# A Mamba-style layer with an expert FFN: both batches' scans as one stream of 64 chunks, with projection, normalisation and output stage as side work at fixed chunks

## The chip, the cores and the metric

The kernel runs on one core of one Trainium2 chip. The metric is the device time of one execution in microseconds. Of the kernel before there are three timed runs, and one more execution was profiled.

## What is computed

x is (2, 2048, 128) in fp32, two batches of 2048 tokens. A small vector per batch (the modulation) gives shifts, scales and two gates ga and gb, whose magnitude is at least 0.25.

```
h = layernorm(x) * (1 + ca) + sa
zxbcdt = h @ in_proj_w.T                     # z 256, x 256, B 64, C 64, dt 2
per direction (forward, and backward on the reversed sequence):
    xBC = silu(causal_conv4(xBC)); dt = softplus(dt + dt_bias); A = -exp(A_log)
    state = state * exp(dt * A) + dt * x B^T;  y = C state + D * x    # per head
    y = y * silu(z);  y = y * rsqrt(mean(y*y) + eps) * norm_w
x = x + ga * ((y_fw + y_bw) @ out_proj_w.T)
h = layernorm(x) * (1 + cb) + sb
expert = argmax(h @ gate_w.T + gate_b + expert_bias)              # of 8
x = x + gb * (relu(h @ w1[expert] + b1) @ w2[expert] + b2)
```

## The kernel before, in words

Everything is one function, `build`, with one instruction list per engine written out by hand: SP issues loads, POOL is GpSimd, ACT ScalarE, PE TensorE, DVE VectorE. Each engine runs its list in order; an instruction that needs another's result waits on a counting semaphore (`wait_ge`). There is no scheduler: the order of the calls in the loops is the order of the work.

The sequence of a batch is cut into 16 chunks of 128 tokens, and four chunks make a block (512 tokens) or, in the scan, a step. A batch is scanned backwards first and then forwards, so it has 32 chunks in 8 steps. For each of the two batches, three phases follow one another, and each ends in `phase_end` (L325), at which all four engines drain and wait for each other:

- Phase 0, normalisation and projection. DVE takes statistics of all 16 chunks (L1075, L1078), POOL the power -1/2 (L477), DVE normalises (L1086), PE transposes (L809), ACT modulates (L606), PE projects to x, B and C (L819) and to z and dt (L825), DVE copies the former to `raw` (L1096), ACT takes silu of z (L617). Then come softplus (L1109 to L1131), the sums of decays (L832, L835), their exponentials (L626) and a split into three bf16 parts, `eparts` (L1147 to L1154). At the head of the second batch POOL also cuts b2 into parts (`cut_b2`, L449) before it does anything for phase 0.
- Phase 1, the scan. Convolution by step: for the two x groups ACT writes the first tap to PSUM banks 1 and 7 (`tap0`, L645) and DVE adds three (`taps`, L1168), the two banks in alternation; for B and C ACT and POOL do it in SBUF in two alternating accumulators (L636, L498, L503). ACT takes the tanh (L653, L656), DVE multiplies (`gate_bc` L1174, `gate_x` L1181), ACT copies C (L662). Per chunk: POOL makes `lseg` (L486); PE `prepare` (L847) transposes x and B and makes the score and decay matrices; ACT takes `decays` (L683), `tokens_major` (L673, L675) and `squares` (L691); DVE does `mix` (L1193, L1196), `carry` of the state (L1210) and `gate_y` (L1236); PE `scan` (L874) makes the new state's part in bank 6 and y in bank 4 or 5. PE is one chunk ahead: `prepare(q + 1)`, then `scan(q)`. `xt` and `bs` have three buffers (TM, L148).
- Phase 2, the output, in four blocks: ACT scales the forward part (L732), DVE adds the backward part (L1248), PE transposes (L915), ACT copies (L740), PE projects (L924), DVE multiplies by ga (L1301) and adds x (L1307), takes statistics (L1310, L1313), POOL the power (L549), DVE normalises (L1319, L1323), POOL shifts (L551), PE transposes (L951), ACT copies (L759), PE makes the gate's logits (L958), DVE chooses an expert (`choose`, L1261 to L1269), PE counts ranks (L934, L935), DVE computes each token's row (`place`, L1280 to L1291), and POOL scatters the four chunks of a block by four indirect DMAs (L538).

After both batches come tables of what each expert got (L1340 to L1363, padding rows by L569), and then the FFN: 39 tiles of 128 rows, loaded by expert, with L984 and L1001 as its matmuls and an indirect store (L582). The change leaves that part as it is, but for its place in memory.

PSUM banks are given by phase: in the scan 0 for transposes, 1 and 7 for the convolution, 2 and 3 for scores, 4 and 5 for y, 6 for the state.

## Time and profile before

| | us |
|---|---|
| three timed runs | 640.8, 639.4, 640.35 (median 640.35) |
| the profiled execution, its own time | 637.29 |
| its span, first to last instruction | 635.4 |
| mean granted TensorE clock | 0.802 of full speed |
| busy in the span: PE, DVE, POOL, ACT | 421.7, 395.9, 301.4, 270.9 |

The time of an execution holds some 1.9 us more than the span of its instructions. Terms of a sum are taken from the profiled execution, and the sum is set beside 637.29 before it is set beside the median. The page gives busy time by engine; a view by stage gives the same for stretches of the span, with the granted clock (1.00 is 2.4 GHz, 0.50 is 1.2); the view by line gives the mean duration of an instruction and, where neighbours overlap on an engine, a busy time that is less than count times mean.

### The profile page before, as it was taken

Reading aid. Unit: us, or ns where it says so; the run is one execution under the profiler, and the core shown is the slowest. Engines: PE = TensorE matmul, PEld = TensorE weight load, DVE = VectorE, ACT = ScalarE, POOL = GpSimd, SP = SyncE. Lnnn points to the kernel's source line nnn. Section 1 sums busy time; section 2 is a strip of 40 time slices with the busy share of each in tenths; the row PEclk is TensorE's granted clock in tenths of the full one; section 3 lists DMA queues with packets and bytes.
Section 4 is the critical chain, followed back from the end, with each engine's and each line's share of the span. In section 5 each row is a group of like instructions: output and inputs, shape, how many; then the busy total and the mean of one; then the engine's idle time right before and its main releaser. Section 6 shows DMA issues by size and latency. Waiting matters only on the chain.

```text
span 635.4 us, 9951 instructions
## 1 busy us (share of the span) xinstructions
PE 421.7 (66%) x2798; PEld 360.9 (57%) x2798; DVE 395.9 (62%) x1240; ACT 270.9 (43%) x777; POOL 301.4 (47%) x453
## 2 busy tenths in 40 slices
PE   0329329998998575306627999999667310799994
PEld 0116218877887474204416878788556310799994
DVE  0365476888884474524556888886476424387884
ACT  1014456777774421003626777775521000344441
POOL 7410087656643154472037666672125454165664
PEclk9959658999999755557956999999875555699997
DMA  8300000000000001000000000000000014488780
GB/s 221 132 1 0 1 1 2 1 1 2 1 2 2 0 26 42 34 34 0 1 1 0 2 2 1 2 2 2 1 1 34 34 68 123 131 231 229 210 237 26
DMA packets 20789, 29.16 MB, mean 46 GB/s; under 512 B 4076, under 2 KB 13548, under 8 KB 20608
## 3 DMA queue, kind: packets, MB, share of 16 engines
q1 hardware_dynamic: 17520, 20.98, 11.9%
q0 software_dynamic: 3216, 7.56, 3.3%
q8 instruction: 23, 0.38, 0.3%
q14 instruction: 30, 0.25, 0.1%
HBM read 20.97 MB, written 8.01 MB: 46 GB/s over the span
## 4 chain that ended last, share of the span: by engine, by line
PE 27%; DVE 25%; POOL 14%; issue 14%; ACT 10%; DMA 4%; POOLq 2%; SPq 2%; DVEq 0%; ACTq 0%
DVE bank L1168 6%; PE bank L819 4%; POOL routed_rows L538 3%; DVE ms L1193 3%; DMA out_dram<-arena 2%; ACT bank L645 2%; DVE st L1210 2%; POOLq L327 2%; PE bank L984 2%; PE bank L825 2%; POOL out_dram L582 2%; PE bank L870 2%; DVE bc L1174 2%; PE bank L890 2%; ACT es L683 2%
## 5 line engine op out<-in xcount | busy, mean ns | idle before, releaser
L486 POOL TENSOR_SCALAR lseg<-strict,av 128x128 f32<-128x128 f32 x128 | 46.9, 380 | 69.3 <-PE bank L870 69.3
L1168 DVE SCALAR_TENSOR_TENSOR bank<-arena,cw,bank 128x512 f32<-128x512 f32 x96 | 65.8, 746 | 5.7 <-ACT bank L645 5.7
L498 POOL TENSOR_SCALAR prod<-arena,cw 128x512 f32<-128x512 f32 x48 | 33.2, 691 | 74.5 <-DVEq L327 73.7
L1193 DVE SCALAR_TENSOR_TENSOR ms<-es,dtv,bank 128x128 f32<-128x128 f32 x128 | 38.7, 343 | 37.4 <-ACT es L683 37.4
L582 POOL DMA_INDIRECT out_dram<-arena x39 | 38.4, 985 | 36.2 <-DVE arena L1399 16.0
L858 PE MATMUL bank<-ident,cx 128*128 128x128 f32 x128 | 26.0, 287 | 30.3 <-ACT cc L663 27.6
L883 PE MATMUL bank<-xt,bs 128*128 128x128 f32 x240 | 38.4, 284 | 9.9 <-DVE st L1210 9.9
L1001 PE MATMUL bank<-w2s,arena 128*128 x312 | 43.9, 285 | 0.0
L984 PE MATMUL bank<-arena 128*128 128x128 f32 x312 | 42.9, 282 | 0.0
L767 ACT ACTIVATE arena<-bank 128x128 f32<-128x128 f32 x39 | 10.8, 277 | 72.5 <-PE bank L973 70.6
L538 POOL DMA_INDIRECT routed_rows<-rows,rowat x32 | 31.8, 993 | 19.8 <-issue 14.9
L683 ACT ACTIVATE es<-bank 128x256 f32<-128x256 f32 x64 | 24.6, 385 | 38.3 <-PE bank L870 37.7
L870 PE MATMUL bank<-incl,lseg 128*128 128x128 f32 x256 | 40.7, 284 | 0.0
L858 PEld LDWEIGHTS bank<-ident,cx 128*128 128x128 f32 x128 | 16.9, 145 | 40.9 <-issue 32.9
L890 PE MATMUL bank<-xt,skip 128*128 128x128 f32 x256 | 40.1, 280 | 0.0
L894 PE MATMUL bank<-xt,ms 128*128 128x128 f32 x256 | 39.9, 279 | 0.0
L984 PEld LDWEIGHTS bank<-arena 128*128 128x128 f32 x312 | 39.6, 199 | 0.0
L1376 DVE TENSOR_SCALAR arena<-bank,arena 128x128 f32<-128x128 f32 x78 | 23.8, 346 | 24.9 <-PE bank L984 24.7
L883 PEld LDWEIGHTS bank<-xt,bs 128*128 128x128 f32 x240 | 32.5, 196 | 11.9 <-issue 11.9
L1001 PEld LDWEIGHTS bank<-w2s,arena 128*128 128x128 f32 x312 | 38.8, 196 | 0.5
L898 PE MATMUL bank<-st,cs 128*128 128x256 f32 x128 | 38.5, 382 | 0.0
L870 PEld LDWEIGHTS bank<-incl,lseg 128*128 128x128 f32 x256 | 35.6, 201 | 0.0
(223 smaller groups left out, 1203.3 us busy)
## 6 DMA issues: line engine op xcount, KB each, us to landing
arena<-in_w_dram SPq DMA_DIRECT2D x39, 258.0 KB, 3.5
arena<-routed_rows SPq DMA_DIRECT2D x39, 130.0 KB, 3.1
xs<-in_u_dram SPq DMA_DIRECT2D x4, 512.0 KB, 5.7
w2s<-in_w_dram SPq DMA_DIRECT2D x1, 2048.0 KB, 8.5
out_dram<-arena POOLq DMA_INDIRECT x39
routed_rows<-rows,rowat POOLq DMA_INDIRECT x32, 2.5
arena<-in_wmod_dram SPq DMA_DIRECT2D x1, 384.0 KB, 3.9
b2r<-in_b_dram SPq DMA_DIRECT2D x1, 384.0 KB, 9.2
```

Of the source, the lines that this page charges most:

```text
L486: last = pool.tensor_scalar(lseg[:, q % 2, h, :], strict[:, d, :], av[:, col(d, h, t)], 1.0, ALU.mult, ALU.mult)
L538: pool.indirect_dma_start(routed[:, :], bass.IndirectOffsetOnAxis(ap=rowat[:, k, :].bitcast(mybir.dt.uint32), axis=0), rows[:, k, :], None ...
L582: pool.indirect_dma_start(out_rows, bass.IndirectOffsetOnAxis(ap=tok[:, s % 4, :].bitcast(mybir.dt.uint32), axis=0), ob[:, s % 4, :], None ...
L858: pe.transpose(tx[:, h * HD:(h + 1) * HD], cx[:, s % 2, h, c0:c0 + P], ident[:, :])
L870: last = pe.matmul(sg[:, h * P:(h + 1) * P], lseg[:, q % 2, h, :], incl[:, d, :], start=False, stop=True, skip_group_check=True)
L883: last = pe.matmul(sn[:, h * HD:(h + 1) * HD], bs[:, q % TM, h].rearrange("p g n -> p (g n)"), xt[:, q % TM, h * HD:(h + 1) * HD], start=T ...
L890: pe.matmul(ys[:, h * HD:(h + 1) * HD], skip[:, d * NH + h, :], xt[:, q % TM, h * HD:(h + 1) * HD], start=(h == 0), stop=False, skip_group ...
L894: pe.matmul(ys[:, h * HD:(h + 1) * HD], ms[:, q % 2, h, :], xt[:, q % TM, h * HD:(h + 1) * HD], start=False, stop=False, skip_group_check= ...
L984: mm = pe.matmul(bank[2 + 2 * (s % 2) + f // 2][:, c0:c0 + P], w1b[:, s % RW, f * P:(f + 1) * P], hTs[:, s % 2, :], start=True, stop=True)
L1001: last = pe.matmul(y, hr[:, s % 2, f * P:(f + 1) * P], w2s[:, bass.ds(e, 1), f, :].rearrange("p a c -> p (a c)"), start=False, stop=(f == ...
L1168: dve.scalar_tensor_tensor(out=pacc[g][:, :], in0=raw[:, g, c0:c0 + BLK], scalar=cw[:, d, g, k:k + 1], in1=pacc[g][:, :], op0=ALU.mult, op ...
L1193: dve.scalar_tensor_tensor(out=ms[:, q % 2, h, :], in0=es[:, q % 2, h, :], scalar=dtv[:, col(d, h, t)], in1=sg[:, DI:DI + P], op0=ALU.mult ...
```

## The change

The chunks of both batches are numbered 0 to 63 and steps 0 to 15, and there is one loop over all of them. `phase_end` is left once only, ahead of the tables. What were phases 0 and 2 become side work that each engine does between chunks, at places fixed by step S and chunk j of the step:

- Blocks 0 and 1 of the first batch are projected ahead of the loop; 2 and 3 in steps 0 and 1; the second batch's in steps 6 to 9. The statistics of the second batch stand in steps 2 and 3 of the first, its softplus, sums and splits in steps 4 to 6. Statistics go by block (with one small power of -1/2 each) rather than by batch. `hT` has four buffers, not two, and dt is made for all 16 chunks at once.
- The output of a block is spread over three steps: forward norms, `forward`, `both`, `y_turn`, `out_proj`, `residual`, `second_deviation` in the step after its chunks; `second_norm`, `shift`, `h2_turn`, `logits`, `choose`, `ranks`, `place` in the next; `scatter` in the third. The last blocks' is done after the loop. Only two rounds of `rows` exist, as before, but each block's four scatters count on one semaphore.
- All side products of PE go through banks 6 and 7 in turn, in an order that a function lists (`side_order`); PE waits before use u for the reader of use u - 2 (`take`).
- The convolution's x groups go one after the other through bank 1 alone, B and C through one accumulator. `gate_x` is in two halves, chunks apart. The state's part shares bank 4 or 5 with y, so that `carry(Q)` waits for all of y(Q). TM is 2.
- ACT, not DVE, copies `raw`. silu of z is tanh(z/2) on ACT and (1 + t) z on DVE (twice silu; a factor 1/4 in the norm and 1/2 in the weights undo it). ga is multiplied into the output weights, so that L1301 is gone.
- At the start, DVE fills constants that POOL filled; SP loads c_t, half of the first batch, wmod, the other half, the projection weights, nine small operands, then the second batch and w2. The gates of the rows move into step 1, cut_b2 into step 3.

The diff is long; its core, new functions and the loops' order:

```diff
+def proj_at(S):
+    b, s = divmod(S, STEPS)
+    if s < 2:
+        return NBLK * b + s + 2
+    if s >= 6 and b + 1 < B:
+        return NBLK * (b + 1) + s - 6
+    return None
+def gate_at(S):
+    return 1 if S == 0 else proj_at(S - 1)
+def out_at(S, lag):
+    b, s = divmod(S - lag, STEPS)
+    if S < lag:
+        return None
+    if s > NBLK:
+        return NBLK * b + s - NBLK - 1
+    return NBLK * b - 1 if s == 0 and b >= 1 else None
...
+        def side(u):
+            return bank[6 + u % 2]
+        def take(eng, u):
+            if u >= 2:
+                eng.wait_ge(s_free[u % 2], u // 2)
...
-        TM = 3
+        TM = 2
...
-        pacc = (bank[1], bank[7])
...
         @block.gpsimd
+            for Q in range(NCH):
+                S, j = divmod(Q, BT)
+                b, s = divmod(S, STEPS)
+                if Q + 2 < NCH:
+                    decay_rows(Q + 2)
+                if j == 0 and out_at(S, 0) is not None:
+                    forward_norms(out_at(S, 0))
+                if j == 0 and S + 1 < NSTEP:
+                    taps_bc(S + 1, 1)
+                if j == 1 and S + 1 < NSTEP:
+                    taps_bc(S + 1, 0)
+                if j == 3 and S + 2 < NSTEP:
+                    raw_bc_there(S + 2)
+                    taps_bc(S + 2, 2)
...
+                if s in (2, 3) and b + 1 < B and j in (0, 2):
+                    reciprocal_deviation(NBLK * (b + 1) + 2 * (s - 2) + j // 2)
+                if j == 3 and out_at(S, 0) is not None:
+                    second_deviation(out_at(S, 0))
+                if j == 0 and out_at(S, 1) is not None:
+                    shift(out_at(S, 1))
+                if j == 0 and out_at(S, 2) is not None:
+                    scatter(out_at(S, 2))
+                if S == 3 and j == 2:
                     cut_b2()
+            scatter(LASTG - 2)
+            shift(LASTG - 1)
+            forward_norms(LASTG)
+            second_deviation(LASTG)
+            scatter(LASTG - 1)
+            shift(LASTG)
+            scatter(LASTG)
+            phase_end(pool)
...
         @block.scalar
+            for Q in range(NCH):
...
+                if Q + 1 < NCH:
+                    tokens_major(Q + 1)
+                    decays(Q + 1)
+                if Q >= 1:
+                    squares(Q - 1)
+                if S + 1 < NSTEP:
+                    if j == 0:
+                        tanh_x(S + 1, 0)
+                    if j == 1:
+                        tap0_x(S + 1, 1)
+                    if j == 2:
+                        tanh_bc(S + 1)
+                        tanh_x(S + 1, 1)
+                        two_c(S + 1)
+                if A is not None and j == 0:
+                    keep_raw(A, 2)
+                    keep_raw(A, 0)
+                if S + 2 < NSTEP and j == 2:
+                    tap0_bc(S + 2)
+                if S + 2 < NSTEP and j == 3:
+                    tap0_x(S + 2, 0)
...
         @block.tensor
...
+            def scan(Q):
...
+                ys = bank[4 + Q % 2]
+                sn = ys[:, DI:2 * DI]
...
+            for Q in range(NCH):
...
+                A, A1, g, g1 = proj_at(S), gate_at(S), out_at(S, 0), out_at(S, 1)
...
+                if Q + 1 < NCH:
+                    prepare(Q + 1)
+                scan(Q)
+                if A is not None and j == 0:
+                    project(A, 2)
+                    project(A, 0)
+                if A is not None and j == 1:
+                    project(A, 1)
+                if g1 is not None and j == 1:
+                    h2_turn(g1)
+                if A1 is not None and j == 1:
+                    project_z(A1, 0)
+                if g is not None and j == 2:
+                    y_turn(g, 0)
+                    y_turn(g, 1)
+                if g1 is not None and j == 2:
+                    logits(g1)
+                if g is not None and j == 3:
+                    out_proj(g)
+                if g1 is not None and j == 3:
+                    ranks(g1)
+                if A1 is not None and j == 3:
+                    project_z(A1, 1)
...
         @block.vector
+            def carry(Q):
+                dve.wait_ge(s_ys, Q + 1)
...
+            def taps_x(S, g):
...
+                X = NH * S + g
                 for k in (2, 1, 0):
...
+                    if k == HALO - 1:
+                        dve.wait_ge(s_tap0, X + 1)
+                    else:
+                        dve.wait_ge(s_tap, HALO * X + HALO - 1 - k)
+                    dve.scalar_tensor_tensor(out=bank[1][:, :], in0=raw[:, g, c0:c0 + BLK],
...
+            for Q in range(NCH):
...
+                if S + 1 < NSTEP and j == 0:
+                    taps_x(S + 1, 0)
+                if S + 1 < NSTEP and j == 1:
+                    gate_x(S + 1, 0)
+                if Q + 1 < NCH:
+                    mix(Q + 1)
+                carry(Q)
+                if S + 1 < NSTEP and j == 2:
+                    gate_bc(S + 1)
+                    gate_x(S + 1, 1)
+                gate_y(Q)
+                if S + 1 < NSTEP and j == 1:
+                    taps_x(S + 1, 1)
+                if S == 1 and j == 3:
+                    gates_of_rows()
...
+                if g1 is not None and j == 0:
+                    second_norm(g1)
+                if g is not None and j == 1:
+                    both(g)
+                if A1 is not None and j == 1:
+                    gate_z(A1, 0)
+                if g1 is not None and j == 2:
+                    choose(g1)
+                if g is not None and j == 3:
+                    residual(g)
+                if g1 is not None and j == 3:
+                    place(g1)
+                if A1 is not None and j == 3:
+                    gate_z(A1, 1)
```

## Rows read from the trace of the kernel before

**Rows 1.** The profile's page, busy us by engine, share of the span, instructions

```profile
PE 421.7 (66%) x2798; PEld 360.9 (57%) x2798; DVE 395.9 (62%) x1240; ACT 270.9 (43%) x777; POOL 301.4 (47%) x453
```

**Rows 2.** Busy time by stage: stretch, its length, each engine, granted clock, DMA share, GB/s

```profile
0.00:36.00 36.00, 5.10 (x12) 3.03 (x12) 9.45 (x42) 2.98 (x4) 20.23 (x47) 0.94 0.52 156
36.00:81.00 45.00, 24.99 (x90) 15.93 (x90) 24.41 (x97) 16.17 (x45) 3.14 (x2) 0.73 0.00 1
...
90.40:204.90 114.50, 108.03 (x792) 91.66 (x792) 91.41 (x222) 80.61 (x245) 68.14 (x107) 0.96 0.01 1
...
277.00:287.50 10.50, 0.00 (x0) 0.00 (x0) 4.26 (x32) 0.00 (x0) 9.12 (x11) 0.50 0.00 0
287.50:327.00 39.50, 24.47 (x90) 15.75 (x90) 19.93 (x64) 16.11 (x44) 3.11 (x2) 0.76 0.00 1
327.00:336.60 9.60, 0.00 (x0) 0.00 (x0) 6.09 (x10) 5.79 (x9) 8.64 (x12) 0.50 0.00 0
...
451.30:517.00 65.70, 34.61 (x160) 31.20 (x160) 35.30 (x133) 13.81 (x30) 25.13 (x31) 0.58 0.07 25
```

**Rows 3.** Busy time in four chunks of the first loop, columns as above

```profile
116.50:130.50 14.00, 13.15 (x103) 11.16 (x102) 12.33 (x30) 10.74 (x33) 8.62 (x15) 1.00 0.00 1
```

**Rows 4.** The second batch's output stage in order of time: start, us, engine, line

```profile
452.05 1.70 ACT L732 ACTIVATE cx<-arena,rn 128x256 f32<-128x256 f32 x4 [0.17 <-ACTq L327]
...
473.46 0.19 DVE L1261 TENSOR_TENSOR lg<-bank,gb_sum 128x32 f32<-128x32 f32 x1 [0.19 <-PE bank L958]
...
479.40 1.24 POOL L538 DMA_INDIRECT routed_rows<-rows,rowat  x1 [1.26 <-issue]
...
519.62 0.96 POOL L538 DMA_INDIRECT routed_rows<-rows,rowat  x1 [0.30 <-issue]
...
523.30 0.17 DVE L1340 TENSOR_TENSOR count<-nextrow,region 128x8 f32<-128x8 f32 x1 [8.30 <-POOL arena L565]
```

**Rows 5.** The start and the first phase 0 in order of time

```profile
15.43 0.20 ACT L596 ACTIVATE csil<-ct_in 128x2 f32<-128x2 f32 x1 [13.35 <-DMA arena<-in_wmod_dram]
...
66.55 0.29 DVE L1109 TENSOR_TENSOR arena<-dtr,biasb 128x32 f32<-128x32 f32 x2 [1.53 <-ACT dtr L618]
...
80.66 0.22 DVE L1154 CAST eparts<-arena 32x128 bf16<-32x128 f32 x1
```

**Rows 6.** PE's matmuls of the start and of a projected block, in order of time

```profile
24.58 0.98 PE L794 MATMUL bank<-csil,arena 128*128 128x2 f32 x4 [24.58 <-DVE arena L1029]
...
57.24 2.74 PE L819 MATMUL bank<-hT,wx 128*128 128x512 f32 x6
...
59.82 1.90 PE L825 MATMUL bank<-wz,hT 128*128 128x258 f32 x8
```

**Rows 7.** Groups by line: count, busy us, mean ns, idle before and its releaser

```profile
L1168 DVE SCALAR_TENSOR_TENSOR bank<-arena,cw,bank 128x512 f32<-128x512 f32 x96 | 65.8, 746 | 5.7 <-ACT bank L645 5.7
L1181 DVE SCALAR_TENSOR_TENSOR cx<-cx,bank 128x512 f32<-128x512 f32 x32 | 20.4, 675 | 0.0
L1096 DVE COPY arena<-bank 128x512 f32<-128x512 f32 x24 | 16.6, 692 | 16.7 <-PE bank L819 16.7
L1301 DVE TENSOR_TENSOR acc<-bank,row 128x512 f32<-128x512 f32 x8 | 5.5, 687 | 7.8 <-PE bank L924 7.8
L740 ACT ACTIVATE acc<-bank 128x512 f32<-128x512 f32 x16 | 8.7, 595 | 24.8 <-PE bank L915 24.8
```

**Rows 8.** Single lines: duration in ns, least, median and most, first and last start

```profile
L1174 DVE SCALAR_TENSOR_TENSOR bc<-bc,acc x8: 695/1292/1302, 88.1 to 418.6; 128x512 f32<-128x512 f32 x8
L1248 DVE SCALAR_TENSOR_TENSOR cx<-arena,rn,cx x32: 471/479/1487, 207.9 to 479.6; 128x256 f32<-128x256 f32 x32
L503 POOL TENSOR_TENSOR acc<-acc,prod x24: 1259/1272/1817, 81.8 to 408.4; 128x512 f32<-128x512 f32 x24
```

**Rows 9.** PE in order of time: the transposes that open the second and third chunk

```profile
94.39 0.69 PE L858 MATMUL bank<-ident,cx 128*128 128x128 f32 x2 [1.16 <-ACT bs L675]
...
100.21 0.38 PE L858 MATMUL bank<-ident,cx 128*128 128x128 f32 x2
```

More of the change, by code:

```diff
@@ L56, in build @@
+USE = {}
+for _key in side_order():
+    USE[_key] = len(USE)
 def build(nc, u, w_xbc, w_zdt, conv_w, conv_b, dt_bias, a_log, d_skip, norm_w, w_out, gate_w, gate_b,
@@ new lines, in _ @@
+            modulate(0)
+            modulate(1)
+            act.wait_ge(s_scaled, 1)
+            keep_raw(0, 2)
+            tap0_bc(0)
+            keep_raw(0, 0)
+            tap0_x(0, 0)
+            keep_raw(0, 1)
+            modulate(2)
+            for g in (2, 0, 1):
+                keep_raw(1, g)
+            modulate(3)
+            act.wait_ge(s_pmod, 2)
+            for b in range(B):
+                last = act.activation(row[:, b, :, :], bank[2 + b][:, :].rearrange("p (k c) -> p k c", k=4), ACT.Copy)
@@ new lines, in h2_turn, with logits @@
+            def h2_turn(g):
+                u = USE["h2", g]
+                take(pe, u)
+                pe.wait_ge(s_h2, g + 1)
+                for j in range(BT):
+                    last = pe.transpose(side(u)[:, j * P:(j + 1) * P], rows[:, (g % RB) * BT + j, 0:DM], ident[:, :])
+                last.then_inc(s_full[u % 2], 1)
+            def logits(g):
+                u = USE["lg", g]
+                take(pe, u)
+                wait_free(pe, USE["h2", g])
+                for j in range(BT):
+                    last = pe.matmul(side(u)[:, j * NE:(j + 1) * NE], h2c[:, j, :], gw[:, :], start=True, stop=True)
+                last.then_inc(s_full[u % 2], 1)
@@ new lines, in ranks @@
+            def ranks(g):
+                u = USE["rk", g]
+                take(pe, u)
+                pe.wait_ge(s_hot, g + 1)
+                V = BT * NE
+                hv = hot[:, g % 2].rearrange("p j e -> p (j e)")
+                pe.matmul(side(u)[:, 0:V], strict[:, 1, :], hv, start=True, stop=True)
+                pe.matmul(side(u)[:, V:2 * V], ones[:, :], hv, start=True, stop=True).then_inc(s_full[u % 2], 1)
+            pe.wait_ge(s_csbc, 1)
+            pe.wait_ge(s_mod, 32)
+            for m in range(2):
+                last = pe.matmul(bank[0][:, m * B:(m + 1) * B], wm[:, m * DM:(m + 1) * DM], csil[:, :], start=True, stop=True)
@@ new lines, in _ @@
+            last.then_inc(s_pmod, 1)
+            pe.wait_ge(s_const, 2)
+            turn(0)
+            for b in range(B):
+                last = pe.matmul(bank[2 + b][:, :], csil_bc[:, b, :], wm[:, 2 * DM:6 * DM], start=True, stop=True)
+            last.then_inc(s_pmod, 1)
+            turn(1)
+            pe.wait_ge(s_win, 32)
+            for g in (2, 0, 1):
+                project(0, g)
+            turn(2)
+            for g in (2, 0, 1):
+                project(1, g)
+            turn(3)
```

1684 lines of the change are left out of this document (924 added, 760 removed).

## The prediction

> **What bounds the kernel now.** I read the page's busy line first [rows 1]: no engine passes 66% of the span, so what is lost lies between the stages, and the next view has to be the one by stage [rows 2]. There the kernel falls into two kinds of stretch. The chunk loop of a batch (90.4 to 204.9 us, and again 336.6 to 451.3) has PE busy 108.0 of 114.5 us and DVE 91.4, at a granted clock of 0.96: it is bound by PE, with DVE close behind. Everything else is bound by latency. The start takes 36 us, the first projection 45 us (PE busy 25.0), the convolution that opens the first loop 9.4 us (81 to 90.4). After that loop come an output stage of 72 us (204.9 to 277), 10.5 us in which POOL cuts b2 and PE does nothing, the second projection (39.5), its opening convolution (9.6), and, after the second loop, an output stage of 65.7 us with PE busy 34.6 and DVE 35.3 at a clock of 0.58. The tables and the FFN fill the rest. In the loop, a stretch of four chunks is 14.0 us long, with PE busy 13.15, DVE 12.33, ACT 10.74 and POOL 8.62 [rows 3]. So each engine has some room there, DVE and PE least.
>
> **The change, part by part.** The end of the kernel is untouched: from the first instruction of the tables, at 523.3 us [rows 4], to 635.4 is 112.1 us before and after. I sum four stretches.
>
> *Start to the first chunk.* The first chunk's transposes start at 90.4 us before [rows 2]. SP now issues only a quarter of x ahead of wmod, and x of the second batch behind the nine small loads, for which ACT's first modulation and the conv scaling wait. Before, ACT got its first input at 15.4 us [rows 5]; I keep that, since the small loads still end the queue. Then follow: a table load and the modulation of the first blocks, to 18.5; the projection of two blocks and the transposes of the third and fourth at half clock, 9.5 us (six matmul passes took 2.74 us at full clock [rows 6], so about 4 at half); 16 two-pass matmuls for the step sizes, 32 passes at 0.25 us = 8 (four such passes took 0.98 us [rows 6]); the softplus chain, the decay sums and the last part of eparts, 66.55 to 80.9 = 14.4 [rows 5]; DVE's skip and pad fills, 1.5; and 4 for ACT and DVE work woven between (the gates of z, first taps, the Ln table). Sum 56 us. Bounds: 48, if the steps weave perfectly; 65, if the convolution stays in series, its 9.4 us added. POOL's 20.2 us of constants [rows 2] hide beside this chain: part of them goes to DVE's memsets and part behind the first taps; uncovered, what stays ahead of the first taps would be some 10 us.
>
> *The stream of 64 chunks.* DVE has: two loops' work, 2 x 91.4 = 183, and the second opening convolution, 6.1 [rows 2]. Seven of eight output blocks: 35.3 / 4 = 8.8 each, less the multiplication by ga that is now in the weights (0.69, L1301 [rows 7]), 8.1 x 7 = 57. The second batch's normalisation, softplus and splits: 4.3 + 19.9 [rows 2] less 12 copies of raw, half of 16.6 [rows 7], that go to ACT: 16. The gates of z, 14 operations like L1181 at 0.64 to 0.68 [rows 7]: 9.5. The gates of the rows, about 5. The conv taps now go one after the other through one bank: a tap takes 0.746 alone while 96 take 65.8 together (0.686 each), because neighbours overlap; serial with a wait, 0.78, so 96 x 0.09 = 9. And contention for the port, below, 10. Sum 296 us.
>
> PE has 2 x 108 less about 4 for the second warming, 212; projections of six blocks, 2.74 + 1.90 [rows 6] = 28; the step sizes and sums, 7; seven output blocks at 8.65 each at clock 0.58 [rows 2], which at full clock is about 5: 36. Sum 283 us. ACT has 2 x 80.6 + 5.8 and 24 for output [rows 2], 18 raw copies and 14 tanhs of z at 0.6 like L740 [rows 7], 20, and 7 for modulation, softplus and two table loads: 218 us. POOL 2 x 68.1 + 8.6, 44 for output, 9 for cutting b2, 5 for deviations: 203 us. So DVE becomes the fullest engine. The side work is uneven: steps 11 and 12 have none, steps 6 to 8 have both an output block and a projection. Taking in each step the larger of PE and DVE adds some 8 us, mainly in the first and fifth step where PE leads: 304 us.
>
> No engine reaches its sum. The loop of before reached 108/114.5 = 0.94 [rows 2]; the output stage, where the same chain of side work stood alone, 35.3/65.7 = 0.54. The stream has the chain hidden behind chunks, so it is nearest to the first, but pays for this: every side result goes through banks 6 and 7 in turn, and PE waits in order at each for the reader of two uses ago; behind a PE that waits stands the next chunk's preparation, for which ACT and then DVE wait. POOL issues four scatters, each 0.96 us and 0.30 of issue [rows 4], ahead of a chunk's lseg. TM falls from 3 to 2, and carry waits for all of its chunk's matmuls, since both share a bank; I cost these two at nothing, because before, too, PE finished the chunk before gate_y, and mix for the next chunk covers the wait; without that cover it is some 0.5 us a chunk, 32 us. I take 0.88: 304/0.88 = 346 us; ends 323 (0.94) and 390 (0.78, two fifths of the way to 0.54).
>
> *Contention between DVE and POOL.* The rows show it: L1174, with both inputs in SBUF, takes 0.695 us alone and 1.29 in the median inside the loop, and L1248 went from 0.48 to 1.49 once when a POOL operation stood beside it; POOL's own L503 went once from 1.27 to 1.82 [rows 8]. L1181, with one input in PSUM, is steady at 0.67 [rows 7]. In the stream, seven blocks bring 5 such DVE operations each, 35, now beside a POOL busy for 60% of the time: 0.6 x about 0.5 = 0.3 us each, the 10 us above; at most 1.0 each, 35. The Trainium skill ("SBUF — State Buffer", Who interferes with whom) says that a DVE instruction with two SBUF inputs and a GpSimd instruction that reads SBUF take a port in turn, the second blocking until the first has ended. By that rule the trace agrees; it speaks against this change, as it sets more such pairs side by side.
>
> *The tail.* Before, from the end of a batch's loop (451.3) to the tables (523.3) is 72 us [rows 2, 4]. Now one block's chain is left, and part of its forerunner. From forward to choose is 452.05 to 473.46 = 21.4 less 0.7 (L1301); choose, ranks, place to the first scatter 6; scatters 5 and drain 2.5 (523.0 less the last scatter's end) [rows 4]; squares and norms ahead, 2.5: 37 us. But POOL's queue stands in the way twice: scatter(5) and shift(6) come ahead of the last block's norms (5 + 1.5), and scatter(6) ahead of its shift (about 4). Sum 47 us. Bounds: 37, and 55 if all waits add.
>
> Sum: 56 + 346 + 47 + 112.1 = 561.1 us of span, against 635.4. Around the span lay 637.29 - 635.4 = 1.9 us: 563.0. The median of the runs stood 0.48% above the profiled execution (640.35 to 637.29): **566 us**.
>
> **The rivals.**
> (a) The chunks take up side work as smoothly as they ran alone (0.94): 323 us, total 543. For it: the fixed places put an output block's four steps into different chunks, and the conv is spread over the step. Against it: fewer buffers. 0.25.
> (b) The port decides: 35 operations wait 1.0 us, not 0.3, and chunks behind them: +25, total 591. 0.12. The Trainium skill's rule named above would bring this about if POOL were always first.
> (c) In-order stalls (0.78): a PE waiting for side banks or lseg behind scatters, 390 us, total 610. For it: the steps with both kinds of side work ask DVE and PE for some 23 us each and POOL for 18. 0.15.
> (d) Slower than before: the clock. If DVE leads, PE has gaps; should the granted clock fall to 0.5 (1.2 of 2.4 GHz) in the stream, a chunk takes 5.8 us of PE (94.39 to 100.21 [rows 9]) where four took 13.15 at full clock, and side work goes from 71 to some 131: 64 x 5.8 + 131 = 502, +156, total 722. It decides the sign once 74/156 = 47% of the stream is at half clock. For it: clock 0.58 in the output stage with PE busy 53%, 0.73 in the projection with 56% [rows 2]. Against it: PE here would be at 283/346 = 82%, gaps short, a slow PE fills its own gaps, and the loop held 1.00 with idle gaps in each step [rows 3]. 0.04.
> A partial form of (d), ending within 0.2% of before, gets 0.01. The forecast, 0.85 to 0.92, keeps 0.43.
>
> **How the numbers follow.** A measurement tells apart some 0.2%. The low end of the range, 527, takes (a) with a start of 48 and a tail of 39; the high end, 612, holds (b) and (c). Outside are (d), the upper part of (c), and a better stream still. Faster 0.43 + 0.25 + 0.12 + 0.15 = 0.95, same 0.01, slower 0.04.
>
> **What would show it.** First transposes of cx at 50 to 62 us; the last gate_y near 402; clock at 0.95 or more between; DVE busy near 296 us of the 346 and ahead of PE; 14 us in steps 11 and 12, some 26 in steps 7 and 8; raw copies on ACT at 0.6; L1174's successor still near 1.2; some 47 us from the last gate_y to the tables, with scatters ahead of the last norms. A stream above 375 us with DVE below 80% means (c); DVE operations with two SBUF inputs above 1 us each, (b); a clock below 0.9 there, (d). If the start is at 90 us again, my first term is wrong.

## The result, and the profile after

The changed kernel takes **622.4 us** (median of 4 runs, 621.2 to 623.9) against 640.6 us of the kernel before on the same chip: a ratio of 0.971, 95% interval 0.968 to 0.975. The forecast was 566 us, the range 527 to 612. The sign was right; the gain was a quarter of the 74 us forecast. The profiled execution's own span is 621.0 us (before: 635.4). Medians in this document are of all four runs of a kernel, while ratios and their intervals leave out one run each of e1 (613.4 us) and i4 (549.0 us) in which the chip granted a lower clock.

The page's busy line of the changed kernel, which answers to [rows 1]:

```profile
PE 448.1 (72%) x2858; PEld 384.1 (62%) x2858; DVE 393.9 (63%) x1219; ACT 277.3 (45%) x751; POOL 298.3 (48%) x451
```

No engine passes 72%: the kernel is still one that waits. PE is busier than before (421.7), and DVE is where it was. Next the view by stage, which answers to [rows 2]; the stretches are divided at the first transposes of the stream, the last gate of y and the first instruction of the tables. Columns: stretch, length, busy time of PE, PEld, DVE, ACT, POOL, granted clock, DMA share, GB/s.

```profile
0.00:53.00 53.00, 28.98 (x95) 18.90 (x95) 34.79 (x122) 21.59 (x34) 25.32 (x49) 0.76 0.34 106
53.00:457.60 404.60, 322.72 (x1994) 271.64 (x1995) 272.48 (x752) 215.95 (x590) 198.12 (x293) 0.86 0.02 8
457.60:509.10 51.50, 14.46 (x71) 13.04 (x69) 15.08 (x69) 4.49 (x10) 18.87 (x24) 0.57 0.09 32
509.10:621.00 111.90, 81.92 (x702) 80.54 (x702) 71.61 (x278) 35.26 (x117) 55.94 (x86) 0.85 0.60 169
```

The four lengths stand against the four terms of the sum: start 53.0 (56 forecast), stream **404.6 (346)**, tail 51.5 (47), tables and FFN 111.9 (112.1). So the whole miss is in the stream: 58.6 of 59.9 us. And it is not in the work: DVE is busy 272 us there (296 forecast), ACT 216 (218), POOL 198 (203), PE 323 at a clock of 0.86 (283 at full clock). One thing differs in kind: PE, at 323 us, and not DVE, at 272, is the fullest engine. What is missing is engines that work at the same time.

Where they wait, the view of the waits from 60 to 440 us tells; five of its rows (engine, line, waited for: us in total, times, longest):

```profile
DVE ms L1507 <- ACT es L874: 58.7, 23, 7.1
DVE st L1522 <- PE bank L1151: 31.8, 25, 2.2
PE bank L1114 <- DVE cx L1485: 29.3, 11, 3.3
PE bank L1125 <- POOL lseg L623: 17.6, 5, 7.0
PE bank L1193 <- ACT yT L905: 11.4, 4, 4.1
```

The largest is DVE's, but es (the decays that ACT takes) in turn waits for PE, so it is passed on; the three waits of PE are where it starts. The first of the three is at the boundary of a step of four chunks (11 of them). This is the timeline there (start, duration, engine, line, then in brackets the idle time before and what ended it):

```profile
359.78 2.33 DVE L1478 SCALAR_TENSOR_TENSOR bank<-raw,cw,bank 128x512 f32<-128x512 f32 x3
359.82 0.61 PE L1125 MATMUL bank<-incl,lseg 128*128 128x128 f32 x4
...
361.60 0.60 PE L1151 MATMUL bank<-st,cs 128*128 128x256 f32 x2
...
362.20 0.60 ACT L845 ACTIVATE cx<-bank 128x512 f32<-128x512 f32 x1 [0.43 <-DVE bank L1478]
...
363.12 0.69 DVE L1491 SCALAR_TENSOR_TENSOR bc<-bc,accb 128x512 f32<-128x512 f32 x1
363.72 0.68 DVE L1485 SCALAR_TENSOR_TENSOR cx<-cx,bank 128x512 f32<-128x512 f32 x1
363.84 0.63 ACT L852 ACTIVATE cc<-bc 64x512 f32<-64x512 f32 x1 [1.04 <-DVE bc L1491]
364.48 0.63 ACT L853 ACTIVATE cc<-bc 64x512 f32<-64x512 f32 x1
...
365.20 0.42 PE L1114 MATMUL bank<-ident,cx 128*128 128x128 f32 x2 [3.00 <-DVE cx L1485]
...
366.68 1.06 PE L1125 MATMUL bank<-incl,lseg 128*128 128x128 f32 x4
```

This is a step without any side work. The second group's taps end at 362.1, its tanh follows, DVE does mix and carry first and then both gates, ACT copies C, and only then can PE begin the next step's first chunk, 3.0 us late. (PE waits there for both gates and for the copy of C. The view names DVE's cx, which was done at 364.4; the copy of C ended last, at 365.1.) Both groups use one bank, so ACT could write the second group's first tap, at 358.35, only after DVE's gate of the first group, at 357.57 to 358.25. Behind the gap the same four matmuls of L1125 take 1.06 us, against 0.61 in the chunk before (at 359.82): PE runs at half its rate for some 3 us. The four chunks from 360.5 to 377.5 us, with this boundary in them, take 17.1 us; four chunks took 14.0 before [rows 3].

The second wait is behind scatters, in the output steps (same columns):

```profile
245.88 1.15 POOL L672 DMA_INDIRECT routed_rows<-rows,rowat  x1 [0.97 <-POOL rows L661]
...
250.04 0.96 POOL L672 DMA_INDIRECT routed_rows<-rows,rowat  x1 [0.30 <-issue]
251.03 0.72 POOL L623 TENSOR_SCALAR lseg<-strict,av 128x128 f32<-128x128 f32 x2
251.81 0.71 PE L1125 MATMUL bank<-incl,lseg 128*128 128x128 f32 x4 [2.63 <-POOL lseg L623]
```

The third (L1193) is the logits' matmul, whose side bank is that of the first output transpose: ACT frees it only after its copy of C. At 259.33 us, for one, PE has waited 2.51 us there.

### The profile page after: what moved, and what is told of

It reads as the page before. It is cut to its first block and busy times, and to the rows that moved or that the text cites. A ratio compares the mean times of both kernels' runs of the same rounds, so it can differ in the third digit from the quotient of the medians.

```text
span 621.0 us, 10187 instructions
## 1 busy us (share of the span) xinstructions
PE 448.1 (72%) x2858; PEld 384.1 (62%) x2858; DVE 393.9 (63%) x1219; ACT 277.3 (45%) x751; POOL 298.3 (48%) x451
## 5 line engine op out<-in xcount | busy, mean ns | idle before, releaser
L587 POOL TENSOR_TENSOR accb<-accb,prod 128x512 f32<-128x512 f32 x48 | 61.1, 1274 | 50.2 <-ACT accb L820 47.0
L1478 DVE SCALAR_TENSOR_TENSOR bank<-raw,cw,bank 128x512 f32<-128x512 f32 x96 | 72.2, 752 | 2.3
L1125 PE MATMUL bank<-incl,lseg 128*128 128x128 f32 x256 | 48.1, 320 | 22.8 <-POOL lseg L623 22.7
L1125 PEld LDWEIGHTS bank<-incl,lseg 128*128 128x128 f32 x256 | 41.6, 231 | 24.4 <-POOL lseg L623 24.4
L751 POOL DMA_INDIRECT out_dram<-raw x39 | 38.3, 981 | 36.1 <-DVE raw L1836 15.2
L1114 PE MATMUL bank<-ident,cx 128*128 128x128 f32 x128 | 27.7, 301 | 35.9 <-DVE cx L1485 29.3
L1522 DVE SCALAR_TENSOR_TENSOR st<-st,etot,bank 128x256 f32<-128x256 f32 x60 | 28.6, 476 | 34.1 <-PE bank L1151 34.0
L1320 PE MATMUL bank<-w2s,raw 128*128 x312 | 43.8, 285 | 0.0
L1013 ACT ACTIVATE raw<-bank 128x128 f32<-128x128 f32 x39 | 10.8, 278 | 73.4 <-PE bank L1292 70.7
L1303 PE MATMUL bank<-raw 128*128 128x128 f32 x312 | 42.9, 282 | 0.0
L1147 PEld LDWEIGHTS bank<-xt,ms 128*128 128x128 f32 x256 | 41.0, 228 | 3.0 <-DVE cs L1510 3.0
L1143 PEld LDWEIGHTS bank<-xt,skip 128*128 128x128 f32 x256 | 42.6, 236 | 0.0
L863 ACT ACTIVATE xt<-bank 128x256 f32<-128x256 f32 x64 | 24.4, 381 | 37.0 <-PE bank L1115 36.8
## 6 DMA issues: line engine op xcount, KB each, us to landing
w2s<-in_w_dram SPq DMA_DIRECT2D x1, 2048.0 KB, 11.4
```

The source lines that it names most:

```text
L587: pool.tensor_tensor(accb[:, :], accb[:, :], prod[:, :], ALU.add).then_inc(s_tapb, 1)
L1114: pe.transpose(tx[:, h * HD:(h + 1) * HD], cx[:, S % 2, h, c0:c0 + P], ident[:, :])
L1125: last = pe.matmul(sg[:, h * P:(h + 1) * P], lseg[:, Q % 2, h, :], incl[:, d, :], start=False, stop=True, skip_group_check=True)
L1143: pe.matmul(ys[:, h * HD:(h + 1) * HD], skip[:, d * NH + h, :], xt[:, Q % TM, h * HD:(h + 1) * HD], start=(h == 0), stop=False, skip_group ...
L1147: pe.matmul(ys[:, h * HD:(h + 1) * HD], ms[:, Q % 2, h, :], xt[:, Q % TM, h * HD:(h + 1) * HD], start=False, stop=False, skip_group_check= ...
L1303: mm = pe.matmul(bank[2 + 2 * (s % 2) + f // 2][:, c0:c0 + P], w1b[:, s % RW, f * P:(f + 1) * P], hTs[:, s % 2, :], start=True, stop=True)
```

## The experiments

All are edits of the changed kernel, timed against the kernel before on the same chip. Ratios are to the kernel before, where the changed kernel has 0.971. The experiments were made in four sets on three chips, and the kernel before had medians of 637.2 to 638.8 us beside them, 640.6 beside the changed kernel. So a difference in us to the changed kernel can hold some 3 us of that; where it matters the ratio is given too. Each span is of one profiled execution:

| kernel | span, us | median, us | ratio, 95% interval |
|---|---|---|---|
| changed | 621.0 | 622.4 | 0.968 to 0.975 |
| e1 scatters spread | 604.6 | 606.6 | 0.942 to 0.953 |
| e2 convolution early | 580.4 | 582.2 | 0.909 to 0.917 |
| e4 logits first | 608.1 | 609.4 | 0.951 to 0.958 |
| e5 three buffers | 619.9 | 622.6 | 0.973 to 0.980 |
| h1 filler | 612.4 | 615.2 | 0.960 to 0.973 |
| h2 e1 and e4 | 592.8 | 594.6 | 0.930 to 0.937 |
| f1 e1, e2 and e4 | 575.1 | 578.3 | 0.901 to 0.910 |
| i1 f1 and ACT order | 550.6 | 553.9 | 0.865 to 0.875 |
| i2 e2 and ACT order | 581.1 | 582.3 | 0.910 to 0.913 |
| i3 ACT order alone | 628.1 | 628.1 | 0.979 to 0.986 |
| f2 f1 and tail order | 568.2 | 569.0 | 0.885 to 0.899 |
| f3 f2 and b2 split | 566.5 | 567.3 | 0.882 to 0.892 |
| f4 f3 and three buffers | 562.9 | 565.5 | 0.882 to 0.890 |
| g1 f4 and lseg first | 561.7 | 564.0 | 0.880 to 0.891 |
| g2 g1 and ACT order | 537.8 | 539.5 | 0.843 to 0.850 |
| i4 g2 and z first | 536.3 | 540.7 | 0.841 to 0.852 |

**One edit each.** First the three waits of PE and the two buffers that I had costed at nothing.

e1, the scatters spread:

```diff
-                if j == 0 and out_at(S, 2) is not None:
-                    scatter(out_at(S, 2))
+                if j < 3 and out_at(S, 2) is not None:
+                    scatter(out_at(S, 2), j, j + 1 if j < 2 else BT)
```

> The changed kernel with one part moved: the four scatter DMAs of a group no longer stand together on POOL at the first chunk of a step, but one at chunk 0, one at chunk 1, two at chunk 2. Theory A (the scatters hold the chunk's lseg back, so that TensorE waits up to 7 us for it, 17.6 us of such waits in the stream): the stream, 404.6 us in the changed kernel, falls by 12 to 20 us, the total to 602 to 610, and the waits of PE for lseg nearly vanish. Theory B (the convolution's deadline holds the stream): these waits are covered by what else is late in those steps, the total moves by less than 5 us. Theory C (contention for the ports of SBUF): no move, 620 to 624.

Measured 606.6 us: the wait was a real loss, 16 us (15 by the ratios), in the range of theory A. What PE waited for lseg fell from 22.7 us (6 times, over the whole stream; one of them lies behind 440 us) to 9.2 (3 times), so it did not nearly vanish, as A had it; the longest left, 6.9 us, stands behind the cutting of b2.

e2, the convolution one chunk earlier, the same edit on POOL, ACT and DVE (DVE's shown; what falls ahead of the first chunk stands before the loop, and DVE's gate of y waits once in each backward step for its own gate of z):

```diff
             for Q in range(NCH):
                 S, j = divmod(Q, BT)
+                Sc, jc = divmod(Q + 1, BT)
-                if S + 1 < NSTEP and j == 2:
-                    gate_bc(S + 1)
-                    gate_x(S + 1, 1)
+                if Sc + 1 < NSTEP and jc == 2:
+                    gate_bc(Sc + 1)
+                    gate_x(Sc + 1, 1)
                 gate_y(Q)
-                if S + 1 < NSTEP and j == 1:
-                    taps_x(S + 1, 1)
+                if Sc + 1 < NSTEP and jc == 1:
+                    taps_x(Sc + 1, 1)
```

> The changed kernel with the whole convolution of the next step (taps, tanh, gates, the copy of C) one chunk earlier on all engines, so that nothing but the wait for its result changes place; as much work as before. Theory B (the step's first chunk waits for the gates that were issued one chunk before it, about 3.5 us and the time at half clock after it in each of 16 steps): the stream falls by 35 to 55 us, the total to 567 to 587, and the waits of PE for DVE's cx, 29.3 us, vanish. Theory A (scatters): under 10 us. Theory C (ports): no move, 620 to 624, as the operations are the same. A rival within B: the gap only moves to the next thing that is late (the carry), and 10 to 20 us are won.

Measured 582.2 us, 40 us less (37 by the ratios) with the same operations: the largest single cause. The wait for cx is gone from the view of the waits, and step 12, which has no side work, is 14.2 us long (17.0). Carry's wait for the scan fell too, from 34.0 us (26 times, over the whole stream) to 14.0 (15 times): more than half of it had been a consequence. The x groups still share bank 1 here, so what the edit gives back is the lead and not the bank; a run with two banks and the old places was not made.

e4, the logits before the output transposes, in PE's order and in the turn of the side banks:

```diff
-                if g is not None and j == 2:
-                    y_turn(g, 0)
-                    y_turn(g, 1)
                 if g1 is not None and j == 2:
                     logits(g1)
+                if g is not None and j == 2:
+                    y_turn(g, 0)
+                    y_turn(g, 1)
```

> The changed kernel with the logits' matmuls before the two transposes of the output stage in the same chunk, so that the logits take the side bank of the second transpose and not that of the first output transpose, which ScalarE frees only behind the copy of C. If the turn of the side banks holds the stream (four waits, 11.4 us): total 609 to 615. If this wait is in the shadow of the late gates: within 3 us of 622.

Measured 609.4 us: 13 us (11 by the ratios) for a wait of 11.4 us, and L1193 no longer waits for ACT. So this was no shadow of the gates.

e5, TM = 3:

> The changed kernel with three buffers instead of two for the token-major copy and the scaled B (two small tables of the decays moved into a buffer that is free by then, to make room). Theory D (ScalarE's copies wait for the scan of the chunk before last, so no engine can run ahead over a late step): the total falls by 10 to 25 us and ACT's waits for ys go. If two buffers are enough, as I had costed it: within 3 us of 622.

Measured 622.6 us: no gain (the ratio, 0.976, is even above 0.971, with intervals that overlap). The third buffer was rightly costed at nothing, in this kernel, and again on top of other edits (f4, below).

**The clock.** h1 fills the gap at the boundary:

```diff
+                if j == 0 and Q > 0:
+                    for _ in range(20):
+                        pe.matmul(sg[:, DI + P:DI + 2 * P], identb[:, :], negm[:, d, 0, :], start=True, stop=True)
                 if j == 0:
                     pe.wait_ge(s_gx, NH * (S + 1))
```

> The changed kernel with 20 filler matmuls (bf16, 128x128, result never read) on TensorE in front of the wait for the gates at each step's first chunk, so that the gap of some 3 us is filled with work and the granted clock should not fall behind it. It separates the wait from the clock that follows it. If the loss at the boundary is the wait alone: no gain, and 0 to 20 us more where the fillers outlast the wait (15 steps, up to 1.3 us each). If the half clock behind the gap costs as much as the gap (PE ran at half rate for some 3 us after it): 10 to 25 us less than 622, with the granted clock of the stream over 0.90 against 0.86.

Measured 615.2 us: 7 us less, with 21 us of work added that nothing uses. That is under the 10 to 25 expected, and it is not clear of noise: by the ratios, 0.967 against 0.971 with intervals that overlap, it is 3 us. The trace says more. At the boundary shown above PE now waits 1.89 us behind the fillers, and the matmuls that follow keep their full rate:

```profile
355.98 1.28 PE L1108 MATMUL bank<-negm,identb 128*128 128x128 bf16 x20
359.15 0.41 PE L1117 MATMUL bank<-ident,cx 128*128 128x128 f32 x2 [1.89 <-DVE cx L1488]
...
360.15 0.61 PE L1128 MATMUL bank<-incl,lseg 128*128 128x128 f32 x4
```

Of seven such waits that were left at 1.2 to 1.9 us, six were followed like this; behind the seventh (374.67 us) and behind two of 2.19 and 2.86 us (190.58 and 339.56) groups of four took 1.06 us again. The stream's granted clock is 0.89 for 0.86, and PE still waited 16.8 us for cx behind the fillers (29.3 without), so the test is only a part of one. What follows is a part answer: the half rate goes at most boundaries where the gap is partly filled, what it costs in time is not settled (3 to 7 us here, perhaps none), and the wait is the larger part, since e2 wins 40 by removing it.

**Do they add?** f1 has all three:

> The changed kernel with the three edits that won singly: the convolution one chunk earlier (40 us), the scatters spread over three chunks (16 us), the logits before the output transposes (13 us). If they are separate waits, they add: 622 - 69 = 553 us, 549 to 557. If they share a queue's lateness (one late step shadows the other): 558 to 568. If one wait replaces the other, 575 or more.

Measured 578.3 us where the sum is 553 (by the ratios 0.906 where it is 0.872). The scatters and the logits, 16 and 13 us alone, bring 4 on top of e2. h2 has these two without the convolution:

> The changed kernel with the scatters spread and the logits first, and the convolution left where it is. Singly the two won 16 and 13 us; on top of the convolution's shift both together won 4. If they overlap only with the convolution's wait: the two add here, 590 to 596. If they overlap with one another (both ended in the same late chunk of the output steps): 600 to 607.

Measured 594.6 us: they add to one another, 28 of 29 us. So something that e2 brings with it had taken their place. In the waits of f1's stream (53 to 413 us) two stand that were nothing and 3.0 us in the changed kernel, and that e2's stream has with the same totals:

```profile
DVE yzf L1552 <- ACT yzf L898: 16.3, 6, 2.8
PE bank L1101 <- ACT raw L787: 10.5, 3, 4.0
```

and ACT's timeline in chunk 1 of an output step shows what it does before that scaling:

```profile
255.25 0.62 ACT L841 ACTIVATE bc<-accb 128x512 f32<-128x512 f32 x1
255.77 0.58 ACT L848 ACTIVATE cx<-bank 128x512 f32<-128x512 f32 x1
258.28 0.63 ACT L855 ACTIVATE cc<-bc 64x512 f32<-64x512 f32 x1 [1.93 <-DVE bc L1496]
258.92 0.63 ACT L856 ACTIVATE cc<-bc 64x512 f32<-64x512 f32 x1
259.57 0.81 ACT L823 ACTIVATE accb<-raw,cb,cw 128x512 f32<-128x512 f32 x1
260.29 1.69 ACT L898 ACTIVATE yzf<-yzf,rn 128x256 f32<-128x256 f32 x4
261.88 0.57 ACT L787 ACTIVATE raw<-bank 128x512 f32<-128x512 f32 x1
```

From 255.25 to 260.29 ACT does the convolution's tanh, the copies of C and a tap, and idles 1.93 us in them for DVE's gate. In the changed kernel that work is in chunk 2; e2 put it into chunk 1, ahead of the scaling for which DVE waits and of the raw copy that frees PE's side bank. i1 reverses this order on ACT and nothing else:

```diff
+                if g is not None and j == 1:
+                    forward(g)
+                if A is not None and j == 1:
+                    keep_raw(A, 1)
                 if Sc + 1 < NSTEP:
...
-                if g is not None and j == 1:
-                    forward(g)
-                if A is not None and j == 1:
-                    keep_raw(A, 1)
```

> The kernel with the three edits (578.3 us, where 553 would be their sum) and ScalarE's order in chunk 1 of a step changed: forward scaling and the copy of the projection ahead of the convolution's tanh and copy of C. Theory E: by moving the convolution a chunk earlier I put 4 to 5 us of ScalarE's work ahead of these two, and this new wait (DVE for the scaling, PE for the side bank) ate the gains of the other edits: 549 to 558. Rival: the gains overlapped in a wait of another engine: 572 to 580.

Measured 553.9 us, 24 less than f1 by four lines moved, and the sum of the three within 1 us (a ratio of 0.870 where their sum is 0.872). Both waits have left i1's view, whose row for the stream is:

```profile
52.80:388.00 335.20, 290.15 (x1994) 245.75 (x1995) 273.05 (x752) 212.69 (x590) 201.95 (x293) 0.92 0.03 9
```

The same 273 us of DVE work as in the changed kernel now stand in 335 us, and PE's same matmuls take 290 us at 0.92 and not 323 at 0.86.

> The changed kernel with the convolution earlier and ScalarE's order changed, scatters and logits as they were. Theory E: the convolution's deadline was worth more than the 40 us seen, which are net of the new wait: 560 to 572 against 582.2. Rival (the new wait is hidden as long as scatters and logits hold those steps): 578 to 584.

Measured 582.3 us, no gain over e2: the rival of that run, and my theory in its strong form fell. With scatters and logits where they were, the late scaling is hidden: PE's wait for lseg is 33.6 us (7 times), against 21.6 in e2. I read it so: the waits in an output step are stacked, and the last one standing takes all, so that ACT's order counts only when the others are gone. The four times (e2, i2, f1, i1) fit this; which wait hid the scaling, the scatters' or the logits', no run tells.

> The changed kernel with ScalarE's order in chunk 1 changed alone (ahead of one tap of 0.8 us, which is all that stands there in it). By theory E nothing, 619 to 624, as the convolution's tanh is in chunk 2 there. If the order itself was late in the changed kernel too: 605 to 615.

Measured 628.1 us, 6 us **more**, which I had in neither branch. The scaling and the copy, some 2.3 us of ACT by the rows above, now stand ahead of the second group's first tap, and the convolution has no time to give there. I take it as a small dose of the same cause as e2 in the other direction; a run that delays the tap in every step was not made.

**The rest.** The tail, on POOL:

```diff
-            scatter(LASTG - 2)
             shift(LASTG - 1)
             forward_norms(LASTG)
+            scatter(LASTG - 2)
             second_deviation(LASTG)
-            scatter(LASTG - 1)
             shift(LASTG)
+            scatter(LASTG - 1)
             scatter(LASTG)
```

> The kernel with the three edits, and GpSimd's order after the last chunk changed: the last but one shift and the last forward norms come before the eight scatter DMAs that they stood behind, the last shift before the scatters of the group before it. Theory: the tail (some 50 us from the last chunk's end to the barrier, in which TensorE waited 10.4 us twice for POOL's rows) is set by GpSimd's queue: 8 to 13 us less than the kernel with three edits. Rival: the tail is set by the chain over the engines, and the scatters only filled its gaps: within 3 us.

Measured 569.0 us, 9 less. In the changed kernel's tail POOL reads

```profile
463.00 1.19 POOL L672 DMA_INDIRECT routed_rows<-rows,rowat  x1 [0.93 <-issue]
...
468.05 1.27 POOL L658 TENSOR_TENSOR rows<-rows,row 128x512 f32<-128x512 f32 x1
...
469.46 1.08 PE L1184 MATMUL bank<-ident,rows 128*128 128x128 f32 x4 [10.35 <-POOL rows L658]
469.54 0.20 POOL L633 TENSOR_SCALAR rt<-ssq 128x4 f32<-128x4 f32 x1
```

with the last block's norms (L633) 12 us behind the last gate of y. With the new order the tail is 43 us and not 52, and the stream is about as long as in f1.

> As the kernel with the tail's order changed, and the cutting of b2 on GpSimd (9.5 us in one piece, lseg behind it) in three pieces at three chunks. Theory: the one step of 32 us owes its length to it, PE waited 9.6 us there: 4 to 7 us less. Rival: a single stall is caught up by the steps behind it, which are held by other engines: within 2 us.

Measured 567.3 us, 2 less, inside the intervals of both. By the timeline the step itself went from 30.5 to 24.0 us, and most of the 6.5 us was lost again in later steps: the rival's outcome.

> As the kernel with b2 cut in pieces, and three buffers of the token-major copy and of the scaled B, which won nothing alone. If it bought nothing only because the gates' deadline was the binding wait, it wins 5 to 12 us now; if two buffers are enough at any pace: within 3 us.

> The fastest kernel so far (565.5 us) with GpSimd's second deviation of the output stage behind the next chunk's decay rows and not ahead of them: GpSimd waits up to 13 us for DVE's statistics in that place with the rows queued behind it, and PE waited 10.8 us in the stream (5 times) for lseg. Theory: these waits go, 4 to 10 us less. Rival: the second norm on DVE is what becomes late in its place: within 2 us, or up to 4 us more.

Measured 565.5 and 564.0 us. Each is 1 to 2 us lower than the kernel it was put on, and neither can be told from none by its interval.

> As the kernel with the decay rows first, and on ScalarE the forward scaling and the copy of the projection ahead of the convolution's tanh in the same chunk, no longer behind it. DVE waited 16.3 us (6 times) for the scaling, PE 10.5 us (3 times) for a side bank that the copy frees. Theory: 5 to 12 us less. Rival: what ends the step's work elsewhere (DVE is 27 us busy in the longest step of 32) sets it: within 3 us.

Measured 539.5 us, 24.5 less than g1, twice what I expected: when I wrote this I did not yet know that the order was what held f1 back. It is the same effect as i1 against f1 (24.4).

> The fastest kernel so far (539.5 us) with the gate projection ahead of the second transposes in chunk 1 on TensorE, on ScalarE and in the turn of the side banks. PE waited 17.8 us (7 times, up to 6.3) for GpSimd's shifted rows there, with the projection queued behind. Theory: 3 to 8 us less. Rival: the transposes are then what holds the scan of the next chunk as before: within 2 us.

Measured 540.7 us, and a ratio of 0.846 as for g2: the same. **g2 is the best kernel, with i4 its equal: 539.5 us**, 0.846 of the kernel before (interval 0.843 to 0.850) and 0.87 of the changed one. The stream and the tail of g2:

```profile
53.10:384.50 331.40, 291.87 (x1993) 246.67 (x1994) 269.62 (x752) 212.17 (x590) 200.68 (x293) 0.93 0.03 9
384.50:427.60 43.10, 14.60 (x71) 13.16 (x70) 15.08 (x69) 4.48 (x10) 18.81 (x24) 0.55 0.11 38
```

## Why the prediction was right and wrong

**The start, the tail and the end** held: 53.0 us for 56, 51.5 for 47 (with scatters ahead of the last norms and of the last shift, as the text had it), 111.9 for 112.1. In the start one premise was off without much effect: ACT had its first input at 6.2 us and not at 15.4, but its first modulation stood behind the small loads until 12.2.

**The work in the stream** held for ACT (216 us for 218), for POOL (198 for 203) and for PE, whose 283 at full clock became 290 in i1 at 0.92. DVE came to 272 for 296, so "DVE becomes the fullest engine" did not come true: in the changed kernel PE stood at 323 us, and in i1 it still led by 290 to 273.

**The failed step is "I take 0.88: 304/0.88 = 346 us".** The quotient came out at 304/404.6 = 0.75, below even the end of 0.78. I had set it between two stretches of the kernel before, by a judgement of which the new one was nearest to. But what lowers it is not smoothness in general; it is orders of issue, which could have been walked through, and the runs price three of them singly: the convolution's place 40 us, four scatters ahead of an lseg 16, the logits' side bank 13. Together 69, more than the 58.6 that the stream lay over. These do not simply add: the three together gave 44 (f1), as the convolution's new place brought a fourth, ACT's order in chunk 1, worth 24 once the others were gone. With all four changed (i1) the stream is 335 us, 11 under my sum, and 304/335 = 0.91.

**Within it, the convolution was costed as occupancy only.** "The conv taps now go one after the other through one bank ... serial with a wait, 0.78, so 96 x 0.09 = 9" is right for DVE's busy time: 90 taps in the stream at a mean of 752 ns, 0.07 each over the 0.686 that I started from. What came with the one bank is that the second group begins only after the first group's gate. I placed its gate, and that of B and C, in chunk 2 of a step, where all had stood in chunk 1, and the result is read by PE within chunk 3. No engine's share shows that. A chain of taps, tanh, gate and copy against its deadline would have: from the taps' start at 359.78 to the copy's end at 365.1 it is 5.3 us, where a chunk takes 3.5.

**Carry and TM at nothing, "without that cover it is some 0.5 us a chunk, 32 us".** TM is confirmed by e5 and f4. Carry did wait 34.0 us over the stream (31.8 in the view above), the very sum; but more than half of it went with the convolution's move (14.0 us in e2, 9.0 in i1), so most of the cover was lost through another cause. What the shared bank of state and y costs by itself no run shows.

**Rival (c), in-order stalls, 610 us, had the mechanism** and named two of its three places, side banks and lseg behind scatters. Its sign came true as well (a stream above 375 us with DVE below 80%: 404.6 us and 67%). The two places are 29 us; the largest, the convolution, it did not name. I gave it 0.15, although the view of its own evidence (four scatters at 0.96 and 0.30 us each against a chunk of 3.5 us) made a stall in each output step likely.

**Rival (b), the port,** is not what happened. The pairs I had counted got cheaper: the gate of bc (L1174 before, L1491 after) fell from 0.94 and 1.15 us in the mean to 0.70, where the text expected it near 1.2. Lines by form of the stream (count, then busy us, mean ns, idle us before):

```profile
L1545 DVE SCALAR_TENSOR_TENSOR yzf<-yzb,rn,yzf 128x256 f32<-128x256 f32 x28 | 12.9, 522 | 0.0
L1491 DVE SCALAR_TENSOR_TENSOR bc<-bc,accb 128x512 f32<-128x512 f32 x15 | 10.5, 697 | 0.0
L1576 DVE TENSOR_SCALAR rows<-rows,mv,rs 128x128 f32<-128x128 f32 x24 | 9.5, 459 | 0.0
L1382 DVE TENSOR_SCALAR xn<-xs,mv,rstd 128x128 f32<-128x128 f32 x16 | 8.1, 571 | 0.0
```

L1545 has some 0.04 us over its 479 ns alone, 1.2 us in all. The contention went to a group that I had left out, the normalisations: 340 ns before, 571 and 459 now. That is 16 x 0.23 + 24 x 0.12 = 6.5 us. My term of 10 us stood on top of the kernel before's own durations. Against these the normalisations bring the 6.5 us, the gate of bc takes back some 5 (15 times 1.04 less 0.70) and L1545 some 0.5 (it was 541 ns in the mean): about 1 us in all. The term was too large and had the wrong operations in it.

**Rival (d), the clock,** stayed partial: 0.86, not 0.5, though under the 0.9 that the text gave as its sign. Where the text argued that gaps are short and would be filled, the timeline shows that a gap of 3 us was followed by about 3 us at half rate; gaps of 2.52 us for cx (at 72.46 and 95.16 us) were, too, with groups of four matmuls at 1.06 us behind them. The clock followed the waits: 0.92 to 0.93 in i1 and g2, without any edit for it.

**"14 us in steps 11 and 12, some 26 in steps 7 and 8"** came out at 19.4 and 17.0, 34.4 and 34.3 us, each from a step's first es to the next step's. The first pair was the cleanest test in my list, as it has no side work to blame. In e2 step 12 takes 14.2; in i1 steps 7 and 8 take 25.6 and 23.7.

## What to carry to other kernels

An engine's share says what a stretch cannot be shorter than; how near it came here was set by orders of issue, and these must be walked through one by one: for each result that another engine reads, count the chain from the last thing that it waits for to its reader, and compare it with the time between the two places in the program. Where a buffer is shared that was two, ask what lead is lost with it and whether an earlier start gives it back: here the taps in one bank cost some 6 us of busy time, and the chunk of lead that went with them was worth 40 us and could be had back with the bank still shared.

When edits that win alone win less together, look for the wait that took their place, and for work that one of them moved ahead of something else on an in-order engine. Here four lines of order on the least busy of the three engines concerned were worth nothing or less at first (i2, i3) and 24 us once the other waits were gone.

## What the runs showed of the hardware that was not expected

One of the operations slowed most beside POOL has a single tensor in SBUF as its input. The normalisation L1382 (128x128, scalars per partition) takes 0.34 us in the median, as before, but beside POOL's cutting of b2 four of them took 4.73 us, where four alone took 1.11:

```profile
129.31 1.11 DVE L1382 TENSOR_SCALAR xn<-xs,mv,rstd 128x128 f32<-128x128 f32 x4
...
148.67 4.73 DVE L1382 TENSOR_SCALAR xn<-xs,mv,rstd 128x128 f32<-128x128 f32 x4
149.00 1.03 POOL L683 CAST b2p<-rows 32x1024 bf16<-32x1024 f32 x1
150.09 1.03 POOL L684 CAST b2p<-rows 32x1024 bf16<-32x1024 f32 x1
151.20 2.11 POOL L686 TENSOR_TENSOR rows<-rows,b2p 32x1024 f32<-32x1024 f32 x1
```

The four DVE operations end at 153.4 us, as the last of these POOL operations does (153.3). The Trainium skill ("SBUF — State Buffer", Who interferes with whom) lists tensor_scalar, with copy and cast, among the operations that can take the port pair shared with GpSimd, when their operands meet the conditions of a 2-port mode. This trace agrees in that the DVE operations were held as long as POOL's ran (no view tells the mode), and I had gone by the sentence there on two SBUF inputs only.
